# Masks turned in two copies, low parts under high ones, and each routing weight spread in one pass over 64 rows

## The reference, cut to what matters

```python
gate_logits = einsum('bsd,ed->bse', x, gate_w)         # 8 experts
topw, sel = top_k(gate_logits, 2)
topw = softmax(topw, axis=1)                           # over the sequence
base_up, base_gate = xt @ w_up.T, xt @ w_gate.T        # 704 hidden
for e in range(8):
    c = sum(where(sf == e, wf, 0.0), axis=1)
    lo_up = 2.0 * (xt @ up_A[e].T @ up_B[e].T)         # rank 16
    lo_gate = 2.0 * (xt @ gate_A[e].T @ gate_B[e].T)
    h_e = silu(base_up + lo_up) * (base_gate + lo_gate)
    mixed_h += c[:, None] * h_e
    lora_down += 2.0 * (c[:, None] * h_e @ down_A[e].T @ down_B[e].T)
out = mixed_h @ w_down.T + lora_down
```

## Time and profile before

| | |
|---|---|
| median of 3 runs | 1437.02 us (1436.83 to 1437.51) |
| profiled execution | 1436.71 us |
| its span, first to last instruction | 1434.9 us |
| TensorE matmul busy | 1389.6 us, 97% of the span, 8164 instructions |
| TensorE weight load busy | 1214.6 us, 85% |
| VectorE / ScalarE / GpSimd busy | 70% / 63% / 65% |
| granted TensorE clock, mean | 0.998 |

### The profile page before, as it was taken

The page is one execution under the profiler, slowest core; times in us unless marked ns, Lnnn a source line. Parts: engine busy times, 40 slices in busy tenths (PEclk is TensorE's granted clock), DMA queues, the critical chain, the costliest instruction groups (busy, mean ns, idle before and its releaser), DMA issues.

```text
span 1434.9 us, 24075 instructions
## 1 busy us (share of the span) xinstructions
PE 1389.6 (97%) x8164; PEld 1214.6 (85%) x8164; DVE 1011.2 (70%) x2207; ACT 903.5 (63%) x1826; POOL 929.6 (65%) x818
## 2 busy tenths in 40 slices
PE   6999999889999999999999999999999988999998
PEld 4778888678999998998999899989999977878886
DVE  6877776867766766766766767766776788766665
ACT  4554443667777877777777767776776764544433
POOL 3665454477777877777777777777777744745543
PEclk9999999999999999999999999999999999999999
DMA  4000001000000000000000000000000030000000
GB/s 172 1 1 1 1 1 52 23 1 9 23 2 8 23 2 8 23 2 8 22 2 9 1 23 9 1 23 1 8 9 1 2 114 1 0 16 1 16 15 15
DMA packets 11415, 23.29 MB, mean 16 GB/s; under 512 B 928, under 2 KB 5024, under 8 KB 11168
## 3 DMA queue, kind: packets, MB, share of 16 engines
q1 hardware_dynamic: 11296, 21.78, 4.5%
HBM read 19.68 MB, written 2.10 MB: 15 GB/s over the span
## 4 chain that ended last, share of the span: by engine, by line
PE 85%; DVE 7%; POOL 4%; issue 2%; ACT 1%; DMA 0%; DVEq 0%; POOLq 0%; ACTq 0%
PE ps L1602 25%; PE ps L1604 25%; PE ps L1603 25%; PE ps L2011 8%; POOL um_l L356 1%; POOL hid_l L356 1%; DVE mixed L1218 1%; DVE hid L1208 1%; POOL w_l L356 0%; POOL mixed_l L356 0%; PE ps L1615 0%; DVE ps L1462 0%; DVE stats L1063 0%; DVE xn L1082 0%; DVE spread L1082 0%
## 5 line engine op out<-in xcount | busy, mean ns | idle before, releaser
L720 POOL TENSOR_SCALAR probs<-probs,inv_sum 128x128 f32<-128x128 f32 (+7 forms) x256 | 197.7, 776 | 210.6 <-DVE inv_sum L1447 210.6
L1462 DVE CUSTOM_DVE_ANT_0 ps<-ps,causal 128x128 f32<-128x128 f32 (+7 forms) x256 | 194.3, 759 | 125.1 <-PE ps L1604 124.7
L999 ACT ACTIVATE probs<-ps,neg_max 128x128 f32<-128x128 f32 (+7 forms) x256 | 189.4, 740 | 136.6 <-DVE neg_max L1462 136.3
L356 POOL TENSOR_TENSOR hid_l<-hid,hid_h 128x512 fp32r<-128x512 f32 x80 | 109.4, 1368 | 184.2 <-ACT hid_h L836 184.2
L2011 PE MATMUL ps<-ident,probs 128*128 128x128 f32 x1152 | 169.9, 274 | 7.6 <-DVE own_l L356 3.1
L704 POOL TENSOR_TENSOR rot_sin<-swapped,rope 128x512 f32<-128x512 f32 x128 | 165.5, 1293 | 17.8 <-ACT swapped L947 10.7
L710 POOL TENSOR_TENSOR rot<-rot,rot_sin 128x512 f32<-128x512 f32 x124 | 160.2, 1292 | 17.8
L2011 PEld LDWEIGHTS ps<-ident,probs 128*128 128x128 f32 x1152 | 133.1, 141 | 24.1 <-issue 3.8
L1602 PE MATMUL ps<-k_h,q_h 128*128 128x384 f32 (+5 forms) x384 | 151.0, 393 | 2.4 <-DVE q_l L356 2.4
L356 DVE TENSOR_TENSOR own_l<-ps,own_h 128x128 fp32r<-128x128 f32 (+3 forms) x256 | 124.0, 484 | 38.4 <-ACT own_h L970 38.4
L1604 PE MATMUL ps<-k_h,q_l 128*128 128x384 f32 (+5 forms) x384 | 131.3, 342 | 0.0
(11 more groups left out here) (202 smaller groups left out, 4396.1 us busy)
## 6 DMA issues: line engine op xcount, KB each, us to landing
w_raw<-attn_w SPq DMA_DIRECT2D x32, 256.0 KB, 2.9
w_in<-ffn_w SPq DMA_DIRECT2D x12, 576.0 KB, 9.2
x_sb<-x_in SPq DMA_DIRECT2D x4, 512.0 KB, 6.2
out<-x_sb SPq DMA_DIRECT2D x3, 512.0 KB, 3.1
rope<-rope_w SPq DMA_DIRECT2D x1, 1024.0 KB, 6.4
w_in<-ffn_w SPq DMA_DIRECT2D x2, 264.0 KB, 4.6
expand_raw<-expand_w SPq DMA_DIRECT2D x2, 256.0 KB, 5.8
out<-x_sb SPq DMA_DIRECT2D x2, 256.0 KB, 2.1
```

Source lines behind the costliest of these rows:

```text
L356: return eng.tensor_tensor(dst, src, high.bitcast(F32), ALU.subtract)
L720: pool.tensor_scalar(probs[s % 4][:, 0:n], probs[s % 4][:, 0:n], inv_sum[:, s % 4:s % 4 + 1], 1.0, ALU.mult, ALU.mult).then_inc(probs_read ...
L999: act.activation(probs[t % 4][:, 0:a * n].rearrange("p (a n) -> p a n", a=a), view, ACT.Exp, bias=neg_max[:, t % 4:t % 4 + 1], scale=-1.0, ...
L1462: dve.tensor_tensor_reduce(out=view, in0=view, in1=causal[:, SEQ - a * n:].rearrange("p (a n) -> p a n", a=a), scale=-SCALE, scalar=HUGE, ...
```

## The change

The mask columns are written into cm_pad twice, side by side, so that the transposes (of 64 columns now) give the masks in rows 0 to 31 of the bank and once more in rows 32 to 63. ScalarE rounds all 64 rows into one tile maskT; VectorE then writes the low part over rows 32 to 63, from the bank's rows 32 to 63. The rows of `expand` for the weights stand in both halves. EX_M1 and EX_D now read rows 0 to 31, and EX_C1 and EX_C2 take rows 0 to 63 in one pass, high and low part at once. Semaphores and the order of the work stay as they are. An unused tile keeps the places of all that lies behind.

```diff
-            maskT_h = sbuf(st, "maskT_h", [P, CHUNK], F32R)
-            maskT_l = sbuf(st, "maskT_l", [P, CHUNK], F32R)
+            maskT = sbuf(st, "maskT", [P, CHUNK], F32R)
+            sbuf(st, "mask_gap", [P, CHUNK])
...
-                act.activation(maskT_h[:], ps[:, bank, :], ACT.Copy).then_inc(mask_high, 1)
+                act.activation(maskT[0:2 * MASK_ROWS], ps[0:2 * MASK_ROWS, bank, :], ACT.Copy).then_inc(mask_high, 1)
...
-                dve.tensor_copy(cm_pad[:, :, 0:MASK_ROWS], cm[:, ds(CT * c, CT), :]).then_inc(cm_padded, 1)
+                twice = cm_pad[:, :, 0:2 * MASK_ROWS].rearrange("p t (k r) -> p t k r", k=2)
+                dve.tensor_copy(twice, cm[:, ds(CT * c, CT), None, :].to_broadcast([P, CT, 2, MASK_ROWS]))\
+                    .then_inc(cm_padded, 1)
...
-                low(dve, maskT_l[:], ps[:, bank, :], maskT_h[:]).then_inc(mask_low, 1)
+                rest = maskT[MASK_ROWS:2 * MASK_ROWS]
+                low(dve, rest, ps[MASK_ROWS:2 * MASK_ROWS, bank, :], rest).then_inc(mask_low, 1)
...
-                    ins = pe.transpose(ps[:, bank, P * tt:P * tt + P], cm_pad[:, tt, :], ident[:])
+                    ins = pe.transpose(ps[0:2 * MASK_ROWS, bank, P * tt:P * tt + P], cm_pad[:, tt, 0:2 * MASK_ROWS], ident[:])
...
-                    pe.matmul(ps[:, banks[e], :], expand[:, e], maskT_h[:], start=True, stop=True).then_inc(spread_done, 1)
+                    pe.matmul(ps[:, banks[e], :], expand[0:MASK_ROWS, e], maskT[0:MASK_ROWS], start=True, stop=True)\
+                        .then_inc(spread_done, 1)
...
-                    pe.matmul(ps[:, banks[e], :], expand[:, e], maskT_h[:], start=True, stop=False)
-                    pe.matmul(ps[:, banks[e], :], expand[:, e], maskT_l[:], start=False, stop=True).then_inc(spread_done, 1)
+                    both = slice(0, 2 * MASK_ROWS)
+                    pe.matmul(ps[:, banks[e], :], expand[both, e], maskT[both], start=True, stop=True).then_inc(spread_done, 1)
...
-        m[2 * EXPERTS + e, EX_C1, :] = 1.0
-        m[3 * EXPERTS + e, EX_C2, :] = 1.0
+        for part in (0, MASK_ROWS):
+            m[part + 2 * EXPERTS + e, EX_C1, :] = 1.0
+            m[part + 3 * EXPERTS + e, EX_C2, :] = 1.0
```

## The result

The changed kernel takes 1441.84 us, the median of 7 runs (1441.55 to 1442.77), against 1436.83 us for the kernel before on the same chip (7 runs, 1436.06 to 1438.67). The ratio is 1.0036, with a 95% interval of 1.0027 to 1.0045, or 3.9 to 6.5 us more. The profiled execution took 1442.23 us with a span of 1440.4, 5.5 us more than the span of before. The forecast was 1440.9. Ratios are of undisturbed executions: one execution of *Both halves in one full pass*, 2039.84 us at a granted clock of 0.62, is left out.

A forecast was written before the change was run, and what follows sets the result against it. TensorE was taken as the bound, busy 1389.6 of 1434.9 us. Stream terms of 3.8 us plus 0.07 for the first head gave +3.85 on 1437.0, so 1440.9 us; own range 1440.0 to 1441.8, wider range 1437.3 to 1442.2.

The forecast's parts named there:

- Removed passes: TensorE, six stream chunks: two weight-spread passes fewer per chunk at 0.23 us each, 2.8 us together; nothing gained in the heads.
- A change of rows: TensorE's dense stream: each switch between full and few rows costs 0.09 + 0.11 = 0.20 us.
- a block: Few-row spreads between full passes in TensorE's stream: two switches of row count, 0.40 us, bounded by 0 and 0.40.
- A (rows cost nothing): TensorE's stream: 512-column passes hide the row switch, so only removed passes and copies count; 1434.5 us, chance 0.08.
- B (only 0.09 paid): TensorE's stream: each row switch costs just 0.09 us, few-row spreads between full passes 0.18; 1437.4 us, chance 0.08.
- C (64 rows free): TensorE's stream: weight spreads of 64 rows pay nothing, route spreads of 32 rows pay; 1436.1 us, chance 0.07.
- Transposes 0.2 faster in c = 0: Four transposes on TensorE: half the columns halve the load-set pitch to about 0.05 us, up to 0.2 us less per chunk.
- M1 and D of c = 0 pinned at nothing: Route spreads in c = 0: 0.2 us later and 0.2 earlier cancel within the wait for VectorE's index search; 0.
- Copy, 0.07 on the chain of c = 1: VectorE's mask copy of 256 elements instead of 128: +0.07 us in c = 1, twice, and once in the first head.
- rival D: Mask copy in c = 1 no longer waits for GpSimd, 0.96 us less, twice; 1438.9 us, chance 0.05.
- VectorE's low part at nothing: VectorE's low part over 32 rows takes 0.68 us like 64 or 128 rows, so nothing was counted.
- the sum: Stream chunks, each twice: +0.34 us in c = 0, +0.81 in c = 1, +0.74 in c = 2; together 3.8 us.

The follow-up runs named there:

- Both halves in one full pass: Against the kernel before: masks copied twice, VectorE makes one 128-row tile of high and low parts, one 128-row pass per weight; 1434.27 us, ratio 0.9985.
- all rows kept: From the changed kernel: transposes, high part and weight spreads use 128 rows everywhere, route spreads in the six stream chunks; 1435.18 us, ratio 0.9987 against before.

## Why the prediction was right, and where it was off

The mechanism and the sign held: few rows in a dense stream cost more than the passes they save. Step by step:

**Removed passes, 0.23 each: right.** Two of them gave 0.40 to 0.45 per chunk with all rows kept (the pitch makes 0.46).

**A change of rows, 0.20, a block 0.40: right,** at 32 and 64 rows and for passes of 512 columns, though it was read from matmuls of 2 and 8 rows. My account of the steps was off in one place, and did not fit my own price: I had a single spread 0.32 behind the full pass, the full pass 0.32 behind it and the next 0.34 behind that, which makes a block of 0.29 (0.98 - 0.69), not 0.40. The second step is 0.43, because the spread's own late load (0.11) and the change back (0.09 to 0.10) meet there. Rivals A (rows cost nothing), B (only 0.09 paid) and C (64 rows free) fall with the rows above.

**Transposes 0.2 faster in c = 0: wrong.** The tile view of the loads, after, and four transposes in c = 1, to be held against the earlier trace rows:

```profile
L1702 PEld LDWEIGHTS ps<-ident,cm_pad x32: 108/111/113, 30.1 to 1336.3; 128*64 128x64 f32 x32
```

```profile
106.14 0.60 PE L1702 MATMUL ps<-ident,cm_pad 128*64 128x128 f32 x4
```

The loads do take 0.111 us (0.141 before), yet the four take 0.60 as they did: the pitch stays (0.60 - 0.27) / 3 = 0.11. I took the load's 0.14 us for what sets the pitch and halved it; it fell by a fifth, and the pitch didn't follow. In c = 0 the shift falls by 0.05 there.

**M1 and D of c = 0 pinned at nothing: off by 0.12,** in part by the same term. Before, M1 started at 52.58, so the pitch would have let TensorE go on at 53.04; it restarted at 53.22, 0.18 later, for VectorE's search. M1 and D are now 0.09 + 0.11 + 0.09 later, and without the 0.2 from the transposes these 0.29 use the slack up and go 0.11 over it. The route spreads alone over 32 rows show that by themselves: 0.09 and 0.11. The restart, VectorE and TensorE in turn, answers to the earlier trace rows:

```profile
53.72 0.16 DVE L1115 FIND_INDEX8 top_at<-top,ps 128x8 uint32<-128x8 f32 x1
```

```profile
53.27 0.73 PE L1708 MATMUL ps<-maskT,expand 32*128 32x512 f32 x2
53.94 0.39 PE L1606 MATMUL ps<-w_h,mixed_h 128*128 128x256 f32 x1
```

It lies 0.22 behind the start of the last search, as before (53.00, 53.22), and 0.67 behind M1, as in c = 1 (0.65): both limits come due together here. The search is held up by VectorE's low part as well (below), so no run here tells which of the two sets the 0.12.

**Copy, 0.07 on the chain of c = 1: right,** 0.07 and 0.10, and 0.08 and 0.04 by itself. The copy still waits for GpSimd, so rival D is out. Tile view and timeline, after, which answer to the earlier trace rows:

```profile
L1170 DVE COPY cm_pad<-cm x8: 278/294/1262, 29.7 to 1328.3; 128x256 f32<-128x256 f32 x8
```

```profile
101.48 1.26 DVE L1170 COPY cm_pad<-cm 128x256 f32<-128x256 f32 x1
```

**VectorE's low part at nothing: the step that failed.** I put it at nothing because durations agree, and they do (0.68 for 32 rows and for 128). What changed is the start. The second head, before and after:

```profile
1202.42 0.17 DVE L1074 TENSOR_SCALAR var_eps<-mean_var 128x4 f32<-128x4 f32 x1
1202.49 0.68 DVE L356 TENSOR_TENSOR maskT_l<-ps,maskT_h 128x512 fp32r<-128x512 f32 x1
1203.10 0.68 DVE L1182 TENSOR_TENSOR part_sum<-ps,spread 128x512 f32<-128x512 f32 x1
```

```profile
1205.11 0.17 DVE L1075 TENSOR_SCALAR var_eps<-mean_var 128x4 f32<-128x4 f32 x1
1205.31 0.68 DVE L357 TENSOR_TENSOR maskT<-ps,maskT 32x512 fp32r<-32x512 f32 x1
1206.03 0.69 DVE L1186 TENSOR_TENSOR part_sum<-ps,spread 128x512 f32<-128x512 f32 x1
```

The starts lie 0.07 and 0.61 apart before, 0.20 and 0.72 after: 0.24 us, and the chain goes over VectorE here, so the head is 0.25 longer. In the stream it is covered, except at the search in c = 0: with all rows kept TensorE waits there 0.26 for it.

**Heads and end.** The first head's 0.35 goes with TensorE's granted clock. Its mean from 28 to 40 us is 0.72 in the trace of after and in three others, and these have nearly all the growth in this head: 0.35, with all rows kept 0.41, with both weight passes over 32 rows 0.74 and over 64 rows 0.30. In before and in the other six the mean is 0.86, and those six grow by -0.02 to 0.08. The low part's start isn't needed for it, since in the two kernels with weight passes the low part starts at row 0. In after, the shift rises from 0.30 to 1.91 at 38.06 under the lower clock, and the waits behind take most of it back. Whether the change brings the lower clock about isn't shown: all four kernels that have it altered the spreads of this head, but so did two of the six that don't, and there is one trace of each. The windows of before and of after (us; busy time and count of PE, PEld, DVE, ACT, POOL; PEclk, DMA share, GB/s):

```profile
36.00:40.00 4.00, 2.61 (x13) 1.73 (x12) 3.85 (x8) 2.13 (x5) 1.33 (x2) 1.00 0.00 0
1430.00:1435.00 5.00, 1.36 (x10) 0.95 (x8) 1.72 (x3) 0.16 (x1) 0.00 (x0) 1.00 0.31 105
```

```profile
36.00:40.00 4.00, 4.00 (x12) 3.05 (x10) 3.44 (x6) 2.59 (x5) 1.75 (x2) 0.53 0.00 0
1435.00:1440.00 5.00, 1.86 (x10) 1.36 (x8) 1.72 (x3) 0.13 (x1) 0.00 (x0) 0.59 0.31 105
```

From 34 to 38 us the clock of after is 0.50, the level of 1.2 GHz, while before is at 1.00, the level of 2.4 GHz, again from 36. From 28 to 32, ahead of the fall, TensorE had been idle about half of the time (busy 0.89 and 1.09 us in the two windows of 2 us), ahead of the fall at the end too (0.79 and 1.19 us from 1430). In before it was as idle, and the clock came back sooner or stayed. So the last matmuls take longer at the end, 0.40 us by the shift; none of the other nine traces has it, so I don't count it as the change's. With that, the 0.35 of the first head and the 0.24 ahead of the copy, some 1.0 of the 5.5 us of the profiled execution are no effect of the change that I can show.

In the stream the sum was thus 3.78 for 3.95 measured. The median lies 0.9 us above the forecast and just above the upper end of its own range (1440.0 to 1441.8), inside the wider one. Its distance from the 1436.83 of before is 5.0 us where the sum had 3.85. Of these 1.15 the runs show the 0.25 of the second head and the 0.17 of the stream; the other 0.7 is open, and the interval of the difference, 3.9 to 6.5, is wide enough to hold it.

## What to carry to other kernels

In a dense stream count changes of the row mode, not rows: an isolated spread of 32 or 64 rows costs 0.40 us more than a full one of 0.23, so zero-padded rows are the cheaper choice, and small ones belong next to each other or behind a wait. Folding two passes into one pays (0.20 to 0.23 us each) as long as the folded pass stays full; here it paid with the tile under it made by an operation that starts at another row, and the traces show the second head and c = 0 cheaper without one. For an operation of another shape compare where it starts after the one ahead and where the next starts, not its duration.

## What the runs showed of the hardware

- A change between 128 rows and 32 or 64 costs 0.09 to 0.10 us ahead of the first pass, whose weight load then starts with it, and 0.11 for that load; the same on the way back. A block of one or two such passes costs 0.37 to 0.41.
- A VectorE operation of 512 columns that starts at row 32 takes 0.68 us like the others, but it begins 0.03 after the one ahead has ended, and holds the next for 0.72 instead of 0.60; 32 rows from row 0, or writing over its own input, do neither.
- Transposes of 64 and of 128 columns have one pitch, 0.11 us, though their loads take 0.111 and 0.141.
